# A Newton attention stage in an order of one period per quad, with scores of four heads in three parts

## The chip, the core and the metric

The kernel runs on one core of one Trainium2 chip. The metric is the device time of one execution in microseconds (us); lower is better. A profile of one execution gives every instruction's start and duration on the engines: PE (TensorE, with PEld for its weight loads), ACT (ScalarE), DVE (VectorE), POOL (GpSimd) and SP (SyncE, which issues DMAs).

## What is computed

The input x has 8 batch rows of 512 tokens of 128 numbers, all float32. First comes an attention of a special kind; then six layers of windowed attention and a feed-forward network, which the change leaves alone. The first part of the reference, cut:

```python
s = einsum('bhnd,bhmd->bhnm', Q, K) * scale        # 16 heads of 8, 512 x 512, causal
lam = s_masked.max(-1) + 1.0
for _ in range(4):                                 # Newton passes
    d = maximum(lam[..., None] - s, EPS)
    w = where(mask, 1 / d, 0)
    f = w.sum(-1) - 1
    fp = -where(mask, 1 / d**2, 0).sum(-1)
    lam = lam - f / fp
p = where(mask, 1 / maximum(lam[..., None] - s, EPS), 0)
o = einsum('bhnm,bhmd->bhnd', p / p.sum(-1), V)
x = x + o.reshape(b, n, d) @ Wo.T                  # with Q, K, V from layernorm(x)
```

## The kernel before

Three functions run one after the other: `stage1` (the part above), `stage2` (the six layers) and `stage3` (copies the result out). Only `stage1` is of interest.

**Tiling.** A batch row is worked off in four *quads* of four heads (32 quads in all). The causal scores of one head, 512 x 512, are kept as four *units* u of 128 query tokens with 128 (u + 1) keys: 128, 256, 384 and 512 columns, 1280 together (`ROW`), in the order `UORD = (3, 2, 0, 1)`. A quad has 4 x 1280 columns on 128 partitions.

**Work of a quad.** TensorE projects queries and keys (`project`, into psM) and ScalarE copies them to qT and kT. TensorE forms lam - s (`differences`, into psD): head h sits in rows 32h to 32h + 8 of qT and kT, so the heads of a quad are in different row groups of the array; the masks are added by bf16 multiplications. VectorE reads the scores into S and takes their minimum (`scores_in`), which gives the first lam. Then four Newton passes: ScalarE takes the reciprocal square root of lam - s, unit by unit, since lam is a bias for each row (`roots`, line 541); GpSimd squares the result of heads 0 to 2 (`squares`, line 646) and ScalarE that of head 3 (line 547); VectorE takes count, mean and variance of 1/d with `bn_stats` (`moments`, line 732), from which both sums follow, and updates lam in seven small dependent steps (`small`, lines 751 to 766). After pass 4 lam is transposed (line 768) and SP sends it by four small DMAs into a row of qT (`send_lam`, line 251), so that TensorE can form the *final* differences with keys on the partitions (line 354). ScalarE takes their root out of psD (`roots_final`, line 556), GpSimd squares it (`weights`, line 651), TensorE multiplies with the values (`weigh`, line 399, into psO), ScalarE copies to oq (line 564), TensorE transposes, VectorE divides (`quad_out`). When the four quads of a row are done, the row turns: transposition of attn, output projection, residual, layer norm for stage 2, transposition, store. The layer norm of the next row's input is done meanwhile.

**Order.** Each engine has one strict queue. `stage1` writes it by *slots*: 24 slots a row; slot s does one pass of one quad (`OFFSET = (0, 5, 8, 13, 16, 21)` gives the slots of score, passes 1 to 4 and final within a quad, 6 slots apart from quad to quad), with the other work placed at slot numbers by hand. psD holds two heads (2 x 1280 columns, five banks), so `differences` runs in two *pairs*, and the second pair waits until the first has been read. W has two buffers (`WBUF`), S four. On VectorE the steps of `small` stand between the statistics of the next pass, one after each unit.

Of the kernel before, what the change touches and what calls it, by code (L numbers as in the profile page):

```python
# [18 lines left out]
P = 128  # L19
# [7 lines left out]
QUAD = 4  # L27
# [35 lines left out]

POFF = ({3: 0, 2: SEQ, 0: SEQ + UNIT[2], 1: 2 * SEQ},
        {1: ROW, 3: 3 * SEQ, 2: 4 * SEQ, 0: 4 * SEQ + UNIT[2]})
KLEN = [SEQ - k * P for k in range(NBLK)]
KOFF = [{k: POFF[i][3 - k] for k in range(NBLK)} for i in range(2)]
# [4 lines left out]
NSLOT = 24  # L74
LAST = ITERS + 1
OFFSET = (0, 5, 8, 13, 16, 21)
SLOTS = {}
for _j in range(NQ):
    for _p in range(LAST + 1):
        SLOTS[(6 * _j + OFFSET[_p]) % NSLOT] = (_j, _p, (6 * _j + OFFSET[_p]) // NSLOT)  # L80
WBUF = {1: 0, 2: 1, 4: 0, 5: 1}
SMALLS = (1, 7, 7, 7, 8)


def stage1(nc, x, consts, w1qk, w1vo, x1d, hist):
    with ExitStack() as ctx:
# [27 lines left out]
        S = sb("S", [P, NQ, QUAD, ROW])  # L114
        W = sb("W", [P, 2, QUAD, ROW])
# [4 lines left out]
        stats = sb("stats", [P, 2, NU, 6])  # L120
        inv = sb("inv", [P, NU])
        lam = sb("lam", [P, NQ, 32])
        lamT = sb("lamT", [P, 4, 32])
# [6 lines left out]
        psD = ps("psD", [P, 2 * ROW])  # L130
# [17 lines left out]
        lam_in = [sem(f"lam_in{i}") for i in range(4)]  # L148
        s_d = sem("s_d")
        s_half = sem("s_half")  # L150
        s_s = sem("s_s")
        s_root = sem("s_root")
        s_rootf = sem("s_rootf")
        s_w = sem("s_w")
        s_w3 = sem("s_w3")
        s_wf = sem("s_wf")
        s_stat = sem("s_stat")
        s_small = sem("s_small")
        s_pv = sem("s_pv")
        s_oq = sem("s_oq")  # L160
        s_turn = sem("s_turn")
        s_rden = sem("s_rden")
        s_attn = sem("s_attn")
        s_m = sem("s_m")
        s_mev = sem("s_mev")
        s_x1 = sem("s_x1")
        s_ln = [sem("s_ln_in"), sem("s_ln_out")]
        s_rs = [sem("s_rs_in"), sem("s_rs_out")]
        s_fix = [sem("s_fix_in"), sem("s_fix_out")]
        s_ap = [sem("s_ap_in"), sem("s_ap_out")]  # L170
        held = {e: sem(f"held1_{e}") for e in ("pe", "act", "pool", "dve", "sp")}

        M_PRO, M_B = 3, 13
        E_PRO, E_B = 3, 12
        FIX = 7

# [3 lines left out]
        def live(b, s):  # L180
            return not isinstance(b, int) or 0 <= b - SLOTS[s][2] < BATCH

        def prev(b, s, passes=range(LAST + 1), buf=None):
            while True:
                b, s = (b, s - 1) if s else (b - 1, NSLOT - 1)
                if isinstance(b, int) and b < 0:
                    return None
                if live(b, s) and SLOTS[s][1] in passes and (buf is None or WBUF[s % 6] == buf):
                    return b, s


        def before(b, s):
            p = SLOTS[s][1]
            return ago(b, s, OFFSET[p] - OFFSET[p - 1])


        def ago(b, s, n, passes=range(LAST + 1)):
            b, s = (b, s - n) if s >= n else (b - 1, s - n + NSLOT)
            if isinstance(b, int) and b < 0 or not live(b, s) or SLOTS[s][1] not in passes:
                return None  # L200
            return b, s

        def rank(b, s, passes, quad=None):
            def fits(t):
                return SLOTS[t][1] in passes and (quad is None or SLOTS[t][0] == quad)
            if isinstance(b, int) and b == 0:
                return sum(fits(t) for t in range(NSLOT) if t < s or not live(b, t))
            return b * sum(fits(t) for t in range(NSLOT)) + sum(fits(t) for t in range(s) if live(b, t))  # L210

        def junk(passes, quad=None):
            return sum(SLOTS[t][1] in passes and (quad is None or SLOTS[t][0] == quad) for t in range(NSLOT) if SLOTS[t][2])

        NEWTON = range(1, LAST)
        FINAL = (LAST,)
        FIRST = (0,)
        ARRAY = (0, LAST)
        SENT = (ITERS,)

        def due(t):
            return t + 1 if SLOTS[t][1] else t + 3.5

        def smalls(b, s):
            ups = [t for t in range(NSLOT) if SLOTS[t][1] < LAST]
            if isinstance(b, int) and b == 0:
                return sum(SMALLS[SLOTS[t][1]] for t in ups if due(t) < due(s) or not live(b, t))
            return b * sum(SMALLS[SLOTS[t][1]] for t in ups) + \  # L230
                sum(SMALLS[SLOTS[t][1]] for t in ups if due(t) < due(s) and live(b, t))

        @block.sync
        def _(sp):
# [11 lines left out]
            def send_lam(b, s):  # L246
                j = SLOTS[s][0]
                sp.wait_ge(s_small, smalls(b, s) + SMALLS[ITERS])
                sp.sem_inc(held["sp"], 1)
                for q in range(4):  # L250
                    sp.dma_start(qT[DH1:P:32, j, :].rearrange("h (u q p) -> h u q p", u=NBLK, q=4)[:, :, q, :],
                                 lamT[32 * q:32 * q + NU, j, :]).then_inc(lam_in[j], 16)

            def store_x1(b):
                sp.wait_ge(s_x1, b + 1)
                sp.sem_inc(held["sp"], 1)
                sp.dma_start(tokens(x1d, b - 1), x1[:, :, :]).then_inc(x1_out, 16)

            def store_h(i, n_ev):
                sp.wait_ge(s_mev, n_ev)  # L260
                sp.sem_inc(held["sp"], 1)
                sp.dma_start(hist[bass.ds(i, 1)].rearrange("a p n -> (a p) n"), houtT[:, :]).then_inc(hist_out, 16)

            def body(b):
                first = isinstance(b, int) and b == 0
                second = isinstance(b, int) and b == 1
                tail = isinstance(b, int) and b == BATCH
                for s in range(NSLOT):

                    t = ago(b, s, 1, SENT)  # L270
                    if t is not None:
                        send_lam(*t)
                    if s == 0 and not first:
                        sp.wait_ge(s_x1, b)
                        sp.sem_inc(held["sp"], 1)
                        sp.dma_start(xres[:, :, :], tokens(x, b - 1)).then_inc(xres_in, 16)
                    if s == 1 and not tail:
                        sp.wait_ge(s_ap[0], b + 1)
                        sp.sem_inc(held["sp"], 1)
                        if isinstance(b, int) and b == BATCH - 1:  # L280
                            sp.sem_inc(xin_in, 16)
                        else:
                            sp.dma_start(xin[:, :, :], tokens(x, b + 1)).then_inc(xin_in, 16)
                    if s == 5 and not first and not second:
                        store_h(b - 2, b * E_B + E_PRO + 1)
                    if s == 23 and not first:
                        store_x1(b)

            body(0)
            body(1)  # L290
            with sp.Fori(2, BATCH - 1) as b:
                body(b)
            body(BATCH - 1)
            body(BATCH)
            store_h(BATCH - 1, BATCH * E_B + E_PRO + 3)
            sp.wait_ge(x1_out, 16 * BATCH + 32)
            sp.wait_ge(hist_out, 16 * BATCH + 32)

        @block.tensor
        def _(pe):  # L300
            def m_free(n_ev):
                pe.wait_ge(s_mev, n_ev)
                pe.sem_inc(held["pe"], 1)

            def project(which, j, n_ev, n_x1=None):
                if n_x1 is None:
                    m_free(n_ev)
                else:
                    pe.wait_ge(s_x1, n_x1)
                    pe.sem_inc(held["pe"], 1)  # L310
                pe.matmul(psM[:, :], wqk[:, which, j, :], hT[:, :], start=True, stop=True).then_inc(s_m, 1)

            def turn_h(n_ev, n_ap):
                pe.wait_ge(s_ap[0], n_ap)
                pe.sem_inc(held["pe"], 1)
                m_free(n_ev)
                for k in range(NBLK):
                    mm = pe.transpose(psM[:, k * P:(k + 1) * P], hin[:, k, :], ident[:, :])
                mm.then_inc(s_m, 1)
# [3 lines left out]
            def differences(b, s, pair):  # L323
                j, p, back = SLOTS[s]
                if pair == 0 and p:
                    pe.wait_ge(lam_in[j], 64 * (rank(*before(b, s), SENT, j) + 1))
                    pe.sem_inc(held["pe"], 1)
                elif pair == 0 and not (j == 0 and isinstance(b, int) and b == 0):
                    pe.wait_ge(s_mev, b * E_B + E_PRO + (2 * j + 1 if j else 0))
                    pe.sem_inc(held["pe"], 1)  # L330
                heads = (2 * pair, 2 * pair + 1)


                def free(i):
                    t = (b, s) if pair else prev(b, s, ARRAY)
                    if t is None:
                        return
# [1667 lines left out]
```

## Time and profile before

| | us |
|---|---|
| median of 3 runs | 5497.16 |
| lowest, highest | 5484.47, 5499.78 |
| the profiled execution, its own time | 5491.38 |
| its span, first to last instruction | 5489.6 |
| busy in the span: PE, DVE, POOL, ACT | 4505.2, 4021.2, 3451.4, 3029.9 |

The span is what the engines saw; a little lies around it. Busy time is a sum over three stages with different limits, so a stage has to be read from stretches of its own. The PE clock is the clock that was granted to TensorE as a share of 2.4 GHz; its levels are 1.2 and 2.4 GHz.

### The profile page before, as it was taken

The numbers are of one execution on the slowest core, as the hardware profiler recorded it, in microseconds if no ns is written. First come the engines' busy times: TensorE is split into PE (matmuls) and PEld (weight loads), VectorE is DVE, ScalarE is ACT, GpSimd is POOL, SyncE is SP. The second block draws the span as 40 slices with busy tenths as digits, with TensorE's granted clock in tenths as the row PEclk, the third lists the DMA queues.
The fourth block names the chain that finished last, engine by engine and source line by source line (L and its number), as shares of the span: only waits on it lengthen the run. The fifth ranks groups of instructions, "written<-read, shape, count | busy, mean of one in ns | idle before, by whom it ended". The sixth has DMA issues, their size and how long they took to land. (4 is left out here: it accounts for less than half of the span.)

```text
span 5489.6 us, 155667 instructions
## 1 busy us (share of the span) xinstructions
PE 4505.2 (82%) x60088; PEld 2421.4 (44%) x60088; DVE 4021.2 (73%) x7142; ACT 3029.9 (55%) x4257; POOL 3451.4 (63%) x1662
## 2 busy tenths in 40 slices
PE   4676666766666658999999899999999899989995
PEld 2333333333333325554555455544555455545553
DVE  6666675656666638887888788878888788878883
ACT  5667676766777634554555444544555455545551
POOL 4556665656656646666666666666666566656662
PEclk9755555555555569999999999999999999999997
DMA  0000000000000014444444444444444444444443
GB/s 11 5 1 8 7 2 7 2 8 0 8 5 2 6 39 115 106 106 109 114 106 108 114 107 104 106 117 98 106 106 105 99 110 109 110 108 115 106 106 86
DMA packets 234292, 382.56 MB, mean 70 GB/s; under 512 B 38433, under 2 KB 63777, under 8 KB 233505
## 3 DMA queue, kind: packets, MB, share of 16 engines
q1 hardware_dynamic: 229408, 371.06, 28.7%
q8 instruction: 488, 8.00, 0.6%
q10 hardware_dynamic: 4224, 2.10, 0.1%
q14 instruction: 172, 1.40, 0.1%
HBM read 51.89 MB, written 18.87 MB: 13 GB/s over the span
## 5 line engine op out<-in xcount | busy, mean ns | idle before, releaser
L732 DVE BATCH_NORM_STATS2 stats<-W 128x6 f32<-128x512 f32 (+3 forms) x2048 | 863.6, 478 | 565.5 <-POOL W L646 565.4
L646 POOL TENSOR_TENSOR W<-W 128x1280 f32<-128x1280 f32 x384 | 881.5, 2319 | 512.8 <-ACT W L541 510.0
L541 ACT ACTIVATE W<-S,lam 128x512 f32<-128x512 f32 (+3 forms) x2048 | 946.6, 551 | 123.7 <-DVE lam L766 90.1
L1557 POOL TENSOR_TENSOR m<-m 128x1024 f32<-128x1024 f32 x384 | 902.5, 2362 | 67.6 <-DVE m L1665 67.4
L1174 PE MATMUL pb<-xs,wg 128*128 128x512 f32 x1536 | 768.4, 635 | 51.4 <-DMA xs<-hist 36.8
L1563 POOL TENSOR_TENSOR sm<-sm,mx 128x1024 f32<-128x1024 f32 x192 | 451.9, 2354 | 511.6 <-DVE mx L1679 511.6
L1688 DVE SCALAR_TENSOR_TENSOR nf<-rn,m 128x1024 f32<-128x1024 f32 x384 | 616.1, 1636 | 99.2 <-ACT rn L1419 76.0
L351 PE MATMUL psD<-kT,qT 9*128 9x384 f32 (+3 forms) x1024 | 410.6, 767 | 322.2 <-DVE S L719 176.0
L1410 ACT ACTIVATE lnn<-pb,cst 128x1024 f32<-128x1024 f32 x192 | 213.8, 1114 | 814.5 <-PE pb L1181 814.5
L1405 ACT ACTIVATE sq<-pb 128x1024 f32<-128x1024 f32 x384 | 381.9, 1021 | 509.8 <-PE pb L1174 509.8
L354 PE MATMUL psD<-qT,kT 9*128 9x512 f32 (+3 forms) x1024 | 407.5, 763 | 266.0 <-ACT WF L556 142.9
L1553 POOL TENSOR_TENSOR sqs<-sq 128x1024 f32<-128x1024 f32 x192 | 456.9, 2379 | 228.3 <-ACT sq L1405 228.3
L1568 POOL TENSOR_TENSOR pr<-pr,rsum 128x1024 f32<-128x1024 f32 x192 | 407.3, 2121 | 306.8 <-DVE rsum L1701 304.4
L1664 DVE TENSOR_TENSOR m<-pb,tab 128x1024 f32<-128x1024 f32 x384 | 464.6, 1210 | 15.5 <-ACT sq L1405 12.4
L1665 DVE TENSOR_TENSOR m<-pb,tab 128x1024 f32<-128x1024 f32 x384 | 465.5, 1212 | 0.0
L351 PEld LDWEIGHTS psD<-kT,qT 9*128 9x128 f32 x1024 | 230.0, 317 | 521.2 <-issue 509.7
L1174 PEld LDWEIGHTS pb<-xs,wg 128*128 128x128 f32 x1536 | 292.9, 201 | 363.7 <-issue 356.7
L651 POOL TENSOR_TENSOR WF<-WF 128x1280 f32<-128x1280 f32 x128 | 294.1, 2319 | 239.5 <-ACT WF L556 239.5
L1181 PE MATMUL pb<-sqs,ones 128*128 128x512 f32 x768 | 394.8, 638 | 29.8 <-DVE m L1665 22.9
L354 PEld LDWEIGHTS psD<-qT,kT 9*128 9x128 f32 x1024 | 228.9, 315 | 416.8 <-issue 405.8
L1230 PE MATMUL pb<-pT,vr 64*64 64x32 f32 x12288 | 335.7, 221 | 65.6 <-issue 65.6
L1246 PE MATMUL pb<-wg,xs 128*128 128x512 f32 x768 | 372.8, 608 | 20.1 <-issue 17.7
(120 smaller groups left out, 7559.2 us busy)
## 6 DMA issues: line engine op xcount, KB each, us to landing
qkn<-nf SPq DMA_DIRECT2D x1536, 128.0 KB, 2.4
vr<-v SPq DMA_DIRECT2D x96, 768.0 KB, 6.0
vr<-v SPq DMA_DIRECT2D x96, 192.0 KB, 5.5
xr<-hist SPq DMA_DIRECT2D x48, 256.0 KB, 2.9
hist<-xo SPq DMA_DIRECT2D x48, 256.0 KB, 4.0
wg<-wqkv SPq DMA_DIRECT2D x24, 384.0 KB, 3.6
xs<-hist SPq DMA_DIRECT2D x48, 128.0 KB
vr<-v SPq DMA_DIRECT2D x96, 64.0 KB, 6.2
```

The source lines that it names most:

```text
L351: pe.matmul(psD[:, c:c + UNIT[u]], qT[r, j, u * P:(u + 1) * P], kT[r, j, 0:UNIT[u]], start=fresh, stop=True, skip_group_check=True)
L354: pe.matmul(psD[:, c:c + UNIT[u]], kT[r, j, k * P:(k + 1) * P], qT[r, j, k * P:SEQ], start=fresh, stop=True, skip_group_check=True)
L541: ins = nc.scalar.activation(W[:, buf, h, c], S[:, j, h, c], ACT.Abs_reciprocal_sqrt, bias=lam[:, j, i:i + 1])
L646: nc.gpsimd.tensor_tensor(W[:, buf, h, :], W[:, buf, h, :], W[:, buf, h, :], ALU.mult).then_inc(s_w, 1)
L732: ins = nc.vector.bn_stats(out=stats[:, buf, i, :], in_=W[:, buf, h, UOFF[u]:UOFF[u] + UNIT[u]])
L1174: mm = pe.matmul(out[:, half, :], wg[:, g, c:c + P], xs[:, 0:SEQ], start=True, stop=True)
L1553: nc.gpsimd.tensor_tensor(sqs[:, :, :], sq[:, :, 0, :], sq[:, :, 1, :], ALU.add).then_inc(s_sqs, 1)
L1557: nc.gpsimd.tensor_tensor(m1[:, which, :, :], m1[:, which, :, :], m2[:, which, ::-1, :], ALU.add)\
L1563: nc.gpsimd.tensor_tensor(x, x, mx[:, :].unsqueeze(2).broadcast_to([P, 16, 64]), ALU.subtract).then_inc(s_sub, 1)
L1664: nc.vector.tensor_tensor(m1[:, which, :, :], src[:, :, :], tab[:, which, 0, :, :], ALU.mult)
L1665: nc.vector.tensor_tensor(m2[:, which, :, :], src[:, :, :], tab[:, which, 1, :, :], ALU.mult)\
L1688: nc.vector.scalar_tensor_tensor(out=nf[:, which, :, :], in0=rn[:, which, :].unsqueeze(1).broadcast_to([P, 2, SEQ]), scalar=1e12, in1=m1[: ...
```

## The change

Only `stage1` and its tables change.

- **Order.** The slots go. The loop body is now written once per quad ("period") on every engine, `for j in range(NQ)`, with each step at a fixed place and a *lag*: `quad(b, j, lag)` is the quad that entered `lag` periods ago. Scores and pass 1 belong to lag 0, passes 2 and 3 and half of pass 4 to lag 1, the rest of pass 4 to lag 2, the final part to lag 3, the row's turn to lag 4. The places are the result of a search over orders.
- **Scores of four heads at a time, in three parts.** `PARTS = ((3,), (2, 0), (1,))`: unit 3 of all four heads (512 columns, a bank each), then units 2 and 0 (384 + 128, a bank each), then unit 1 (256, two heads in a bank, in two halves with a wait on `s_half` between). `take` waits for a bank's last user. `scores_in`, `root_final`, `weights` and `weigh` follow the same parts; `root_final` and `weights` take four heads in an instruction.
- **A buffer per pass.** W and stats have one buffer for each of the four passes; S has two instead of four.
- **Squares.** Pass 4 (`p = 3`) is squared by GpSimd for all four heads; in the other passes ScalarE still squares head 3.
- **Updates.** The steps of an update (`update`) stand behind each other and no longer between statistics.
- **Values** are projected a quad at a time (4 products of 32 columns) and not for the whole row.
- Most work has semaphores of its own (`s_root[p]`, `s_up[p]`, ...) instead of shared ones with computed ranks.

```diff
-NSLOT = 24
-OFFSET = (0, 5, 8, 13, 16, 21)
-WBUF = {1: 0, 2: 1, 4: 0, 5: 1}
+PARTS = ((3,), (2, 0), (1,))
+BANKS = ((0, 1, 2, 3), (4, 0, 1, 2), (3, 4))
+SQP = ((0, 1, 2), (0, 1, 2), (0, 1, 2), (0, 1, 2, 3))
+SQA = ((3,), (3,), (3,), ())
...
-        S = sb("S", [P, NQ, QUAD, ROW])
-        W = sb("W", [P, 2, QUAD, ROW])
+        S = sb("S", [P, 2, QUAD, ROW])
+        W = sb("W", [P, ITERS, QUAD, ROW])
-        psD = ps("psD", [P, 2 * ROW])
+        psD = ps("psD", [P, 5, SEQ])
...
+                if part < 2:
+                    for u in PARTS[part]:
+                        for h in range(QUAD):
+                            unit(h, u)
...
+                else:
+                    for i in range(2):
+                        if i == 1:
+                            pe.wait_ge(s_halff if final else s_half, at(n))
+                            pe.sem_inc(held["pe"], 1)
+                        unit(i, 1)
+                        unit(2 + i, 1)
+                        mask(i, 1, 1)
+                        mm = mask(2 + i, 1, 1)
...
+            def root_final(q, part):
...
+                if part == 0:
+                    ins = nc.scalar.activation(WF[:, :, 0:SEQ], psD[:, 0:4, :], ACT.Abs_reciprocal_sqrt, bias=zero[:, 0:1])
```

One period on ScalarE, and then on GpSimd. The conditions `if live(...)` and `if last(...)` ahead of each step are left out; they only drop steps of quads that do not exist.

```diff
+                        queries(quad(b, j, 0))
+                        root(quad(b, j, 2), 3, 2)
+                        root_final(quad(b, j, 3), 0)
+                        keys(quad(b, j, 0))
+                        root(quad(b, j, 1), 1, 0)
+                        root(quad(b, j, 2), 3, 3)
+                        root(quad(b, j, 1), 1, 1)
+                        turned_attn(quad(b, j, 4))
+                        root(quad(b, j, 1), 1, 2)
+                        root(quad(b, j, 1), 1, 3)
+                        square(quad(b, j, 1), 1, 3)
+                        root_final(quad(b, j, 3), 1)
...
+                        values(quad(b, j, 0))
...
+                        root(quad(b, j, 1), 2, 0)
...
```

```diff
+                        square(quad(b, j, 0), 0, 0)
+                        weights(quad(b, j, 3), 2)
+                        square(quad(b, j, 0), 0, 1)
+                        square(quad(b, j, 0), 0, 2)
+                        square(quad(b, j, 1), 3, 0)
+                        square(quad(b, j, 1), 3, 1)
+                        square(quad(b, j, 1), 3, 2)
+                        weights(quad(b, j, 2), 0)
+                        square(quad(b, j, 0), 1, 0)
+                        square(quad(b, j, 0), 1, 1)
+                        square(quad(b, j, 0), 1, 2)
+                        square(quad(b, j, 1), 3, 3)
+                        weights(quad(b, j, 2), 1)
+                        square(quad(b, j, 0), 2, 0)
...
```

TensorE at the head of the loop, before: the first pair of score blocks of a quad, two heads in turn, unit by unit (the reads name kT and qT; `L342` rows are waits).

```order
L342 ISA
L351 MATMUL psD<-kT,qT 128x512
L342 REGISTER_ALU
L351 MATMUL psD<-kT,qT 128x512
L351 MATMUL psD<-kT,qT 128x384 x2
L351 MATMUL psD<-kT,qT 128x128 x2
L351 MATMUL psD<-kT,qT 128x256
L360 MATMUL psD<-cmaskb,identb 128x128
L360 MATMUL psD<-cmaskb,identb 128x256
```

The same place of the changed kernel: part 0 of the final differences of the quad three periods back (`L371`), the key projection (`L337`), part 0 of the new quad's scores (`L374`).

```order
L371 MATMUL psD<-qT,kT 128x512 x4
L381 MATMUL psD<-cmaskb,identb 128x128 x4
L327 ISA
L337 MATMUL psM<-hT,wqk 128x512
L327 REGISTER_ALU
L363 REGISTER_ALU
L374 MATMUL psD<-kT,qT 128x512 x4
L381 MATMUL psD<-cmaskb,identb 128x128 x4
```

A block of one unit now covers four heads, and blocks of two quads alternate part by part where whole arrays followed each other.

VectorE in the loop, before: statistics of a pass with the update of another quad between them.

```order
L732 BN_STATS stats<-W 128x6
L741 REGISTER_ALU
L754 TENSOR_TENSOR psX<-psX,stats 128x16x2
L732 BN_STATS stats<-W 128x6
L741 REGISTER_ALU
L757 TENSOR_TENSOR psX<-psX,stats 128x16x2
L732 BN_STATS stats<-W 128x6
L741 REGISTER_ALU
L759 TENSOR_REDUCE psX<-psX 128x32
```

The changed kernel, from the reading of part 0 (`L840`) through the statistics and the update of pass 2 to the statistics of pass 4's last head.

```order
L840 TENSOR_SCALAR S,psX<-psD 128x512 x4
L849 BN_STATS stats<-W 128x6 x16
L865 TENSOR_TENSOR psX<-stats,psX 128x16x2
L867 TENSOR_TENSOR psX<-psX,stats 128x16x2
L869 TENSOR_TENSOR psX<-psX,stats 128x16x2
L871 TENSOR_REDUCE psX<-psX 128x32
L873 RECIPROCAL inv<-psX 128x16
L875 SCALAR_TENSOR_TENSOR psX<-psX,inv 128x16
L878 TENSOR_TENSOR lam<-lam,psX 128x16
L849 BN_STATS stats<-W 128x6 x4
```

The seven steps have moved together, behind all sixteen statistics of their own pass.

GpSimd in the loop, before: three squares of a pass (`L646`), then the final weights of a pair of heads (`L651`).

```order
L646 TENSOR_TENSOR W<-W 128x1280
L645 REGISTER_ALU
L646 TENSOR_TENSOR W<-W 128x1280
L650 REGISTER_ALU
L651 TENSOR_TENSOR WF<-WF 128x1280
L650 REGISTER_ALU
L651 TENSOR_TENSOR WF<-WF 128x1280
```

The changed kernel: the weights of part 2, squares of passes 1 and 4, the weights of part 0, squares of pass 2 and the fourth square of pass 4.

```order
L740 TENSOR_TENSOR WF<-WF 128x4x256
L733 REGISTER_ALU
L734 TENSOR_TENSOR W<-W 128x1280
L733 REGISTER_ALU
L734 TENSOR_TENSOR W<-W 128x1280 x4
L739 REGISTER_ALU
L740 TENSOR_TENSOR WF<-WF 128x4x512
L734 TENSOR_TENSOR W<-W 128x1280 x3
L733 REGISTER_ALU
L734 TENSOR_TENSOR W<-W 128x1280
```

The weights come in pieces of four heads and stand between squares of three different passes.

## Rows read from the trace of the kernel before

**Rows 1.** The page: granted clock of TensorE in 40 slices of the span, tenths.

```profile
PEclk9755555555555569999999999999999999999997
```

**Rows 2.** Stretches: start:end length, busy us (count) of PE, PEld, DVE, ACT, POOL; clock, DMA.

```profile
511.50:564.80 53.30, 39.20 (x132) 20.16 (x132) 37.98 (x129) 40.76 (x77) 36.67 (x17) 0.51 0.00 1
...
621.00:691.10 70.10, 44.07 (x156) 24.90 (x156) 37.78 (x134) 42.67 (x81) 36.33 (x24) 0.56 0.04 12
449.80:691.10 241.30, 162.28 (x556) 86.02 (x556) 154.97 (x530) 168.67 (x316) 149.73 (x79) 0.53 0.02 5
2009.50:5489.60 3480.10, 3193.55 (x55616) 1733.17 (x55616) 2775.74 (x2888) 1671.67 (x1729) 2249.27 (x1015) 0.96 0.46 107
```

**Rows 3.** Timeline (start, us, engine, line): ScalarE's first and last copy of oq.

```profile
208.00 0.56 ACT L564 COPY oq<-psO 128x512 f32<-128x512 f32 x1
...
1992.10 0.58 ACT L564 COPY oq<-psO 128x512 f32<-128x512 f32 x1 [7.00 <-PE psO L399]
```

**Rows 4.** Waits in 449.8 to 691.1, one batch row: us in total, times, longest.

```profile
DVE stats L732 <- POOL W L646: 72.8, 25, 9.2
...
ACT qT L497 <- PE psM L311: 13.8, 4, 4.5
ACT vals L506 <- PE psM L414: 12.7, 1, 12.7
ACT W L541 <- DVE lam L766: 10.9, 3, 4.0
```

**Rows 5.** Timeline of ScalarE: keys, final roots, roots of four heads, a square.

```profile
1031.34 0.67 ACT L502 ACTIVATE kT<-psM,fixed 128x512 f32<-128x512 f32 x1
1031.91 2.53 ACT L556 ACTIVATE WF<-psD,zero 128x1280 f32<-128x1280 f32 x2
1034.33 7.34 ACT L541 ACTIVATE W<-S,lam 128x512 f32<-128x512 f32 x16
1041.70 1.27 ACT L547 ACTIVATE W<-W 128x1280 f32<-128x1280 f32 x1
```

**Rows 6.** Timeline of VectorE: scores of two heads begun, sixteen statistics, a whole update.

```profile
1005.20 0.67 DVE L719 TENSOR_SCALAR_CACHE_REDUCE S<-psD 128x512 f32<-128x512 f32 x1
...
1006.95 0.72 DVE L719 TENSOR_SCALAR_CACHE_REDUCE S<-psD 128x512 f32<-128x512 f32 x1
...
1011.32 6.39 DVE L732 BATCH_NORM_STATS2 stats<-W 128x6 f32<-128x512 f32 x16
...
1034.03 0.20 DVE L751 TENSOR_TENSOR psX<-stats,psX 128x32 f32<-128x32 f32 x1
...
1035.57 0.17 DVE L766 TENSOR_TENSOR lam<-lam,psX 128x16 f32<-128x16 f32 x1
```

**Rows 7.** GpSimd: squares in the timeline; a stage 2 group (busy, mean ns | idle).

```profile
1037.86 13.87 POOL L646 TENSOR_TENSOR W<-W 128x1280 f32<-128x1280 f32 x6
...
L1557 POOL TENSOR_TENSOR m<-m 128x1024 f32<-128x1024 f32 x384 | 902.5, 2362 | 67.6 <-DVE m L1665 67.4
```

**Rows 8.** Timeline of TensorE: projection, score blocks, one block alone, masks, values.

```profile
17.91 2.05 PE L311 MATMUL psM<-hT,wqk 128*128 128x512 f32 x2 [0.77 <-ACT hT L497]
...
23.64 4.60 PE L351 MATMUL psD<-kT,qT 9*128 9x512 f32 x14 [0.87 <-ACT kT L502]
...
29.25 1.19 PE L351 MATMUL psD<-kT,qT 9*128 9x256 f32 x2
...
1021.60 0.93 PE L360 MATMUL psD<-cmaskb,identb 128*128 128x128 bf16 x7
...
1040.68 4.50 PE L399 MATMUL psO<-WF,vals 128*32 128x512 f32 x32
```

**Rows 9.** SP and DMA: lam sent, another DMA's landing, first issue of stage 2.

```profile
1027.97 2.27 SPq L251 DMA_DIRECT2D qT<-lamT  x4
...
qkn<-nf SPq DMA_DIRECT2D x1536, 128.0 KB, 2.4
...
2009.50 0.35 SPq L997 DMA_DIRECT2D ident<-consts  x1
```

More of the change, by code:

```diff
@@ L192, in before @@
[L192 to L231, printed above, removed]
+        def quad(b, j, lag):
+            c = j - lag
+            return b * NQ + c, c % NQ, b - (-(c // NQ))
@@ new lines, in live, with last, at, of @@
+        def live(b, j, lag):
+            return not isinstance(b, int) or 0 <= b * NQ + j - lag < QUADS
+        def last(b, j, lag):
+            return (j - lag) % NQ == NQ - 1 and live(b, j, lag)
+        Q_MADE, Q_OUT, K_MADE, K_OUT, V_MADE, V_OUT = range(6)
+        TURNED, TURNED_OUT, SUMMED, ADDED = range(4)
+        def at(n, k=0, per=1):
+            return per * n + (per * NQ + k + 1)
+        def of(r, k=0, per=1):
+            return per * r + (per + k + 1)
+        def norm(r, step):
+            return of(r, step, NORMED + 1)
@@ new lines, in body @@
+            def body(b):
+                for j in range(NQ):
+                    if live(b, j, 0):
+                        send_lam(quad(b, j, 0))
+                    if last(b, j, 1):
+                        store_x1(quad(b, j, 1)[2])
+                        if not isinstance(b, int) or quad(b, j, 1)[2] + 1 < BATCH:
+                            load_xres(quad(b, j, 1)[2] + 1)
+                    if last(b, j, 3):
+                        store_h(quad(b, j, 3)[2])
+                    if j == 2 and (not isinstance(b, int) or b + 2 <= BATCH):
+                        load_xin(b + 2)
@@ new lines, in project, with values @@
+            def project(q, which):
+                n, j, r = q
+                if which == 0 and j == 0:
+                    pe.wait_ge(s_thev, of(r))
+                    pe.sem_inc(held["pe"], 1)
+                pe.matmul(psM[:, :], wqk[:, which, j, :], hT[:, :], start=True, stop=True).then_inc(s_qkv, 1)
+            def values(q):
+                n, j, r = q
+                for k in range(NBLK):
+                    mm = pe.matmul(psM[:, k * 32:(k + 1) * 32], hT[:, k * P:(k + 1) * P], wvo[:, 0, j * 32:(j + 1) * 32],
+                                   start=True, stop=True)
+                mm.then_inc(s_qkv, 1)
@@ L327, in differences, with score @@
+            def score(q, part, final):
+                n, j, r = q
+                if part == 0 and final:
+                    pe.wait_ge(lam_in[j], of(r, 63, 64))
                     pe.sem_inc(held["pe"], 1)
[L328 to L329 removed]
+                elif part == 0:
+                    pe.wait_ge(s_qkv, at(n, Q_OUT, 6))
                     pe.sem_inc(held["pe"], 1)
[L331 removed]
```

986 lines of the change are left out of this document (529 added, 457 removed).

## The prediction

> **What bounds the kernel now.** I read the stretches first, then the waits, then the durations. The kernel has a first stage (stieltjes attention, 8 rows of 4 quads) that ends at 2009.5 us and a second and third stage that take the other 3480.1 us [rows 2, 9]. The diff touches the first stage alone, so 3480.1 us stand, and with them the clock of that part (0.96 granted, against about 0.53 in the first stage, that is the 1.2 GHz level nearly all the time [rows 1, 2]).
>
> In the first stage the copies of a finished quad (oq) come at 208.0 for the first and 1992.1 for the last [rows 3]. One row of four quads takes 241.3 us, 60.3 a quad. In it ScalarE is busy 168.7, TensorE 162.3, VectorE 155.0, GpSimd 149.7 us [rows 2]. No engine is full: even ScalarE idles 72.6 us, 18 a quad. The waits say where [rows 4]: VectorE waits 72.8 us for GpSimd's squares; ScalarE waits 13.8 us for the query projections, 12.7 us for the value projection and 10.9 us for an updated lam. The projections themselves are short (2.05 us [rows 8]); they stand in TensorE's one queue behind score blocks that wait for psD. So the bound is the order in which four strict queues meet, not an engine. The four quads of a row are uneven too: the last one takes 70.1 us, the other three 57.1 in the mean ((241.3 - 70.1) / 3), and a quiet one 53.3 [rows 2].
>
> **The prices.** All from rows.
> ScalarE: 16 root instructions (4 heads) take 7.34 us, 1.84 a head; the square of a head 1.27 [rows 5]. So an instruction costs (1.84 - 1.27) / 3 = 0.19 and a column 0.84 ns. The final roots, two of 1280 columns in 2.53 [rows 5], become pieces of 2048, 512 + 1536 and 1024 columns: 1.92, 2.10, 1.05, sum 5.07, as before (4 x 1.27).
> VectorE: statistics of 4 heads in 6.39, 1.60 a head; reading a head's scores 1006.95 - 1005.20 = 1.75 (the four parts about 0.60, 0.52, 0.25, 0.38); a lam update whose seven steps stand one behind the other 1.71 (1034.03 to 1035.74) [rows 6].
> GpSimd: six squares in 13.87, 2.31 each [rows 7].
> TensorE: a block of 256 columns in one row group takes 1.19 us, that is 3.33 ns a column and 0.34 once. Seven blocks of two heads (1280 and 1024 columns) take 4.60: exactly 1280 x 3.33 ns + 0.34, so the two row groups run side by side, each at its own pace. Masks cost 0.93 for seven [rows 8].
>
> **The change part by part.**
> 1. *Scores of four heads at a time.* A part of 512 columns: 1.71 + 0.34 + four masks 0.6 = 2.7 us; the 384 + 128 part 3.0; the 256 part, in two halves with a wait between, 3.1. Sum 8.8 an array of scores, against two pairs of about 7.3 (4.60 + 0.93 + 1.19 and some 0.6 for the last mask and the seams) = 14.6 before [rows 8]. It saves some 11 us of TensorE a quad; what lies beside it is the work of the other three engines, and TensorE is not in the chain below. That four groups run abreast is not in the rows for row groups; the nearest row is the product with the values, where four column groups take 4.50 us for 1280 columns each (1280 x 3.33 ns + 0.24) [rows 8].
> 2. *Pass 4 squared by GpSimd alone.* ScalarE loses 1.27 us a quad, GpSimd gains 2.31. ScalarE: 168.7 / 4 = 42.2, minus 1.27: 40.9 a quad. GpSimd: 37.4 + 2.3 = 39.7.
> 3. *Updates no longer interleaved with statistics.* VectorE: 16 x 1.60 + 4 x 1.75 + 4 x 1.71 = 39.4, plus about 2.4 for the transposition, the output of a quad and the norms (estimate, from the 38.7 a quad that the row holds now): 41.8 a quad. This step costs VectorE about 3 us; before, the steps hid between statistics.
> 4. *A buffer per pass, the new orders.* They remove nothing and set the period. I laid one period out, zero being ScalarE's query copy. ScalarE: copy, root (pass 4, head 2) to 2.4, final root of part 0 to 4.4, keys 5.1, root (pass 2, head 0) 6.9, root (pass 4, head 3) 8.8. GpSimd: square of pass 4 head 2 from 2.5 to 4.8, part 0 of the final weights (2048 columns, 3.7) to 8.5, then three squares of pass 2 to 10.8, 13.1, 15.4. VectorE: statistics of head 2 to 17.0, head 3 to 18.6, update to 20.35. ScalarE, which would be free at 18.0, waits for this lam until 20.4; from there to the end it has ten roots (pass 3 four, pass 1 four, pass 4 two: 18.4), two squares (2.5), the last part of the final root (1.05) and the quad's copy (0.56), 22.6 together: 43.0. With the hand-overs 43.3 us. GpSimd and TensorE fit: the quad's copy ends at 37.9; its transposition 1.1, the query projection 2.1 and the final scores of part 0 (2.7) end at 44.0, 0.7 into the next period, where ScalarE wants them at 2.4.
> So the chain of a period is: root, GpSimd's square, GpSimd's weights, three squares, two statistics, one update, then ScalarE without a gap. It replaces 57 to 60.
> 5. *The row turn.* The residual, the norms' statistics and three copies. Before, a turn costs 70.1 - 57.1 = 13 us over the others; the bound below is nothing. Its longest wait, 12.7 us for the value projection of the whole row, is gone, since each quad now projects its own quarter; residual and norm still pass through all queues in series. So I take 4.8 a row, 1.2 a quad.
> 6. *GpSimd's weights in pieces of four heads.* They cost at least 1.81 ns a column as the squares do (2.31 / 1280); other two-operand work of 1024 columns on GpSimd takes 2362 ns, 2.31 ns a column [rows 7]. That would lengthen part 0 by 1.0 us, on the chain. I take half, 0.5.
> Mean period: 43.3 + 1.2 + 0.5 = 45.0 us.
> 7. *SP's queue.* Each quad sends lam with four DMAs, 2.27 us of issue [rows 9]; SP waits for that update first in each period and only then stores x1 and loads the next rows. Landing is not shown for them; for a DMA of 128 KB it is 2.4 us. The update of pass 4 ends near 35, lands near 40 and is wanted at 41.3: hidden by 1.3 us, and 1.7 more before ScalarE feels it. The loads of x have a whole row.
>
> **The sum.** The first projection starts at 17.9 as before [rows 8]. A Newton pass alone takes 1.84 + 3 x 2.31 + 2 x 1.60 + 1.71 = 13.7. Period 0 (projections, three parts of scores, their reading 7.0, one pass): 33. Period 1 (two passes and the third begun): 36. Period 2: 40. Periods 3 to 31: 29 x 45.0 = 1305. Then the emptying pipeline: 36, 16 and 19. Behind the last copy 2009.5 - 1992.1 = 17.4 [rows 3, 9]. Together 18 + 33 + 36 + 40 + 1305 + 36 + 16 + 19 + 17 = 1520, against 2009.5. Plus 3480.1 is a span of 5000. The profiled execution took 5491.4 with a span of 5489.6, so 1.8 lie around it: **5002 us**. That execution is 5.8 under the median of the runs (5497.2), which is inside their spread.
>
> **The rivals.**
> - *The order closes tighter.* The wait of 2.4 us for lam shrinks, the turn is hidden: ScalarE alone, 41 to 42 a quad. 29 x 3 = 87 less: 4915. For it: its busy time is 40.9. Against it: VectorE needs 41.8 and cannot run ahead.
> - *The four heads take turns on TensorE.* The multiplications would start in program order; each is recorded as two passes, and the second waits for the first in the same row group, so a part of 512 columns takes 4 x 0.85 + 0.85 + 0.34 + 0.6 = 5.2 instead of 2.7. Then keys, scores and their reading enter the chain: about 1.5 a period, 44 in all: 5046. Against it: 4.60 us is what two independent groups give; in turns the same seven blocks would need about 5.4 [rows 8]. The Trainium skill ("TensorE: Matmul & The Clock Gate", section "Step-by-step: what each phase is for") says just that matmuls stay in program order and only weight loads are pulled ahead; by that rule the time would be 5046, by the row 5002. Its section "The mechanism" draws four row groups as starting almost together; the row of 4.60 bears out that part for two groups.
> - *The row turn costs what it costs now,* 13 instead of 4.8: 7.25 rows of 4 periods x 8.2 = 60 more, 5062. For it: the turn still sends two norms through all four queues in series.
> - *The orders close badly.* ScalarE now loses 18 us a quad to waits; if half of that stays, the period is 50 and the time 5002 + 29 x 5 = 5147. For it: both ScalarE and VectorE are then within 3 us of full, and a delay on one is a delay of the other, with strict queues.
> - *Slower: the round trip of lam.* The final scores of a quad stand ahead of the key projection in TensorE's queue. If the DMAs of lam took L us from the update to the scores, the loop update - L - scores 2.7 - final root to update is about 35 + L us. It decides above L = 9 and makes the kernel slower than before from a period of 62, L = 27: 5002 + 29 x 17.5 = 5510. Against it: 2.27 us of issue and 2.4 of landing [rows 9].
>
> **How the numbers follow.** Forecast (period 44 to 46.5) 0.55; tighter 0.08; heads in turns 0.10; costly row turn 0.14; orders closing badly 0.11; lam slower than before 0.02. The range goes from 4925 (the tighter case nearly whole) to 5105 (turn and half of the bad case), and leaves out some 0.17. Within 0.3% (16 us, about what a measurement of this kernel can tell) of before no case lies; I keep 0.01. Faster 0.97, slower 0.02.
>
> **What would show it.** In the new profile: copies of oq 44 to 46 us apart, over 48 at the turns of rows; the first stage ending near 1520; ScalarE above 90% busy with one wait of about 2 us a quad, for lam at pass 3; VectorE near 93%; blocks of 4 heads x 512 columns in 2.1 us (4.6 if they take turns); the weights' part 0 in 3.7 (4.7 by the other price); the second stage 3480 long. A second stage of another length, or ScalarE waiting for TensorE at the final roots, would make the prediction wrong at its base.

## The result, and the profile after

The changed kernel takes 4943.68 us (median of 4 runs, 4938.53 to 4948.72); the kernel before took 5490.82 beside it (4 runs, 5468.62 to 5499.78). The ratio is 0.901, 95% interval 0.898 to 0.904: some 547 us less. The profiled execution took 4938.53 us with a span of 4936.4. The forecast was 5002, in a range of 4925 to 5105: the time lies inside, 58 us under it.

The page of the changed kernel: busy tenths of four engines and the granted clock in 40 slices. The first 12 slices are the first stage.

```profile
PE   3666666666647999899999999899998999899995
DVE  6999999999956888788878888788887888788883
ACT  5999999999953555445544555455544555455441
POOL 4999999999965676666766676567665766576661
PEclk9755555555558999999999999999999999999997
```

From the second slice to the eleventh three engines now stand at 9, and TensorE, still at the 1.2 GHz level there as in [rows 1], at 6. The stretches have the same columns as [rows 2]: a row's turn period, an ordinary period, the row of four quads that begins with them, and the part behind the first stage.

```profile
986.80:1032.40 45.60, 31.23 (x160) 15.95 (x160) 41.73 (x141) 44.18 (x88) 40.67 (x25) 0.57 0.04 12
1032.40:1074.90 42.50, 28.83 (x140) 12.65 (x140) 38.56 (x126) 39.52 (x77) 38.34 (x16) 0.50 0.00 1
986.80:1159.90 173.10, 115.57 (x580) 52.61 (x580) 159.62 (x530) 162.74 (x315) 157.90 (x79) 0.53 0.02 7
1479.40:4936.40 3457.00, 3179.03 (x55616) 1725.73 (x55616) 2775.45 (x2888) 1672.50 (x1729) 2249.30 (x1015) 0.97 0.46 108
```

A row takes 173.1 us where it took 241.3 [rows 2]. ScalarE, VectorE and GpSimd do about the work they did (162.7, 159.6, 157.9 us), so their idle time is what went: ScalarE's from 72.6 to 10.4 us a row. TensorE does 46.7 us less a row; what that is worth, the run `pairs` below shows.

Timeline of ScalarE (start, us): copies of a finished quad, and SP's first DMA issue of the next stage, as in [rows 3] and [rows 9].

```profile
166.49 0.57 ACT L615 COPY oq<-psO 128x512 f32<-128x512 f32 x1
...
1031.94 0.57 ACT L615 COPY oq<-psO 128x512 f32<-128x512 f32 x1
...
1074.38 0.56 ACT L615 COPY oq<-psO 128x512 f32<-128x512 f32 x1
...
1378.16 0.57 ACT L615 COPY oq<-psO 128x512 f32<-128x512 f32 x1
...
1461.26 0.58 ACT L615 COPY oq<-psO 128x512 f32<-128x512 f32 x1 [3.25 <-PE psO L425]
...
1479.44 0.35 SPq L1142 DMA_DIRECT2D ident<-consts  x1
```

Between the first copy and that at 1378.16 lie 28 periods, 43.27 us each; within a row they are 42.4, 42.4, 42.6 and 45.6. The first stage ends at 1479.4 instead of 2009.5: 530.1 of the span's 553.2 us. The other 23.1 us are in code that is the same, 3457.0 instead of 3480.1 [rows 2]. In the traces of all the runs below this part is between 3449 and 3469 us, and by and large it goes with the time in which TensorE stands at 1.2 GHz in it (265 us in the profile before, 221 after, 220 to 247 in the others, from the mean granted clock of this part). The change does not touch this code. Why the profile before is the longest of all here, no run shows; only the 530 us of the first stage are counted for the change below.

The waits in the row from 986.8 to 1159.9 (us in total, times, longest), against [rows 4]:

```profile
ACT W L585 <- DVE lam L878: 7.9, 4, 2.8
...
DVE stats L849 <- POOL W L734: 4.0, 7, 0.6
...
ACT vals L544 <- PE psM L342: 0.9, 2, 0.5
```

VectorE waited 72.8 us a row for GpSimd's squares and waits 4.0; ScalarE's waits for the projections, 26.5 together, are 0.9; what it still waits for is lam, once a quad (7.9 of its 10.4 us). So the wait for lam closes the chain. The timeline of one ordinary period on ScalarE, then VectorE, GpSimd and TensorE (in brackets: the idle time before, and who ended it):

```profile
1037.19 0.57 ACT L530 COPY qT<-psM 128x512 f32<-128x512 f32 x1
1037.66 1.93 ACT L585 ACTIVATE W<-S,lam 128x512 f32<-128x512 f32 x4
...
1041.90 9.16 ACT L585 ACTIVATE W<-S,lam 128x512 f32<-128x512 f32 x20
1051.09 1.27 ACT L592 ACTIVATE W<-W 128x1280 f32<-128x1280 f32 x1
...
1057.55 7.34 ACT L585 ACTIVATE W<-S,lam 128x512 f32<-128x512 f32 x16 [2.38 <-DVE lam L878]
1064.92 1.27 ACT L592 ACTIVATE W<-W 128x1280 f32<-128x1280 f32 x1
1066.13 3.73 ACT L585 ACTIVATE W<-S,lam 128x512 f32<-128x512 f32 x8
```

```profile
1052.41 3.25 DVE L849 BATCH_NORM_STATS2 stats<-W 128x6 f32<-128x512 f32 x8 [0.61 <-POOL W L734]
1055.69 0.21 DVE L865 TENSOR_TENSOR psX<-stats,psX 128x32 f32<-128x32 f32 x1
...
1057.18 0.17 DVE L878 TENSOR_TENSOR lam<-lam,psX 128x16 f32<-128x16 f32 x1
```

```profile
1037.38 4.61 POOL L734 TENSOR_TENSOR W<-W 128x1280 f32<-128x1280 f32 x2 [0.63 <-ACT W L585]
1041.94 3.60 POOL L740 TENSOR_TENSOR WF<-WF 128x2048 f32<-128x2048 f32 x1
1045.50 9.15 POOL L734 TENSOR_TENSOR W<-W 128x1280 f32<-128x1280 f32 x4
```

```profile
1042.16 2.09 PE L374 MATMUL psD<-kT,qT 9*128 9x512 f32 x8 [2.20 <-ACT kT L536]
1044.19 0.61 PE L381 MATMUL psD<-cmaskb,identb 128*128 128x128 bf16 x4
```

From the query copy at 1037.19 the chain runs through the root at 1037.66, GpSimd's square, its weights (3.60 us), three more squares, VectorE's statistics of two heads and one update, to the roots at 1057.55: 20.36 us. Behind that ScalarE has no gap until the next query copy. TensorE's block of four heads by 512 columns takes 2.09 us, the price of one head's 512 columns (512 x 3.33 ns + 0.34 us = 2.05, by the slope of [rows 8]).

### The profile page after: what moved, and what is told of

Same layout as the page of the kernel before. It is cut to its first block and busy times, and to the rows that moved or that the text cites. A ratio compares the mean times of both kernels' runs of the same rounds, so it can differ in the third digit from the quotient of the medians.

```text
span 4936.4 us, 154683 instructions
## 1 busy us (share of the span) xinstructions
PE 4103.4 (83%) x60260; PEld 2147.1 (43%) x60260; DVE 4056.8 (82%) x7132; ACT 2979.7 (60%) x4240; POOL 3516.9 (71%) x1655
## 5 line engine op out<-in xcount | busy, mean ns | idle before, releaser
L734 POOL TENSOR_TENSOR W<-W 128x1280 f32<-128x1280 f32 x416 | 954.9, 2319 | 141.2 <-ACT W L585 139.9
L849 DVE BATCH_NORM_STATS2 stats<-W 128x6 f32<-128x512 f32 (+3 forms) x2048 | 832.4, 478 | 57.6 <-POOL W L734 56.5
L1853 DVE COPY oT<-pb 128x512 f32<-128x512 f32 x384 | 246.6, 683 | 176.5 <-PE pb L1375 176.5
L374 PE MATMUL psD<-kT,qT 9*128 9x512 f32 (+3 forms) x1024 | 201.8, 747 | 191.0 <-DVE S L840 107.3
L1342 PEld LDWEIGHTS pb<-qkn 64*32 64x32 f32 x24576 | 260.3, 105 | 203.0 <-issue 202.2
L1401 PE MATMUL pb<-oT,wo 128*128 128x512 f32 x768 | 344.4, 602 | 1.5 <-DVE oT L1853 1.5
L1375 PEld LDWEIGHTS pb<-pT,v 64*64 64x64 f32 x12288 | 255.8, 135 | 191.8 <-issue 191.8
```

What stands on the lines that cost most here:

```text
L734: nc.gpsimd.tensor_tensor(W[:, p, h, :], W[:, p, h, :], W[:, p, h, :], ALU.mult).then_inc(s_wp[p], 1)
L849: ins = nc.vector.bn_stats(out=stats[:, p, h * NBLK + u, :], in_=W[:, p, h, UOFF[u]:UOFF[u] + UNIT[u]])
L1375: mm = pe.matmul(out[64 * b:64 * b + 64, s, o:o + WIN], src[64 * s:64 * s + 64, k, c:c + DH2], pT[64 * s:64 * s + 64, b, r:r + WIN], start ...
```

## Is the chain the bound? Four runs with work added

Theory A: the period is that chain, and the engines' waits outside it are real slack. Theory B: all three engines are so full that work anywhere lengthens the period. Four kernels add the same operations on data of their own, once a period: a square of 1280 columns on ScalarE, three statistics on VectorE, a product of 512 columns on GpSimd.

```diff
+ nc.scalar.activation(spareo[:, :], spare[:, :], ACT.Square)
+ for i in range(3):
+     nc.vector.bn_stats(out=spare6[:, i, :], in_=spare[:, 0:SEQ])
+ nc.gpsimd.tensor_tensor(sparep[:, :], spare[:, 0:SEQ], spare[:, 0:SEQ], ALU.mult)
```

**slack_all** puts all three where the engines have slack: behind the value copy, behind the statistics of head 2 in pass 4 (`moments(..., 3, 2)`), and behind the weights of part 1.

> The changed kernel with extra work of no use in each period, on three engines: ScalarE squares 1280 columns (1.2 us) between the value copy and the roots of pass 3, VectorE takes statistics of 512 columns three times (1.8 us) at the end of its period, GpSimd multiplies 512 columns (0.9 us) before its squares of pass 3. Theory A (one chain through the three engines sets the period of 42.4 us; ScalarE's wait of 2.4 us for lam, VectorE's waits of 1.2, 0.6 and 0.6 us, GpSimd's wait of 1.3 us are real slack): the period stays at 42.4 to 42.5 us, the total grows by 0 to 10 us, most of it at the turns of rows. Theory B (ScalarE and VectorE are simply full, at 93% busy): a period grows by 1.2 to 1.8 us, the total by 35 to 55 us.

Measured: 4955.5 us, ratio 0.903 [0.902, 0.905], 11.8 us over the changed kernel; the first stage 13.7 longer. That is a little more than the 0 to 10 expected, and not at the turns of rows. The copies of its row:

```profile
1041.42 0.58 ACT L619 COPY oq<-psO 128x512 f32<-128x512 f32 x1
...
1083.88 0.58 ACT L619 COPY oq<-psO 128x512 f32<-128x512 f32 x1
...
1127.95 0.57 ACT L619 COPY oq<-psO 128x512 f32<-128x512 f32 x1
```

One ordinary period is 42.5 as before; the next is 44.1 instead of 42.4, and only this one grows. It is the one in which VectorE also takes the norm statistics of the next row's input. So some 4.2 us of work (1.25, 1.88 and 1.04) is free in three periods of four: theory A, with the slack used up in the fourth, where VectorE has most to do.

**act_chain**, **dve_chain** and **pool_chain** put one of the three each into the chain: the square behind `square(..., 2, 3)`, in ScalarE's stretch behind lam; the statistics between the last `moments` of pass 2 and its update; the product between the weights of part 0 and the three squares.

> The changed kernel; the same extra square of ScalarE (1.2 us) placed a little later, behind the square of pass 3, inside the stretch that theory A counts as chain. Theory A: the period grows by all of it, to 43.6 us, the total by 36 us. A rival chain through GpSimd alone would let it pass for less than 10 us.

> The changed kernel; the same three extra statistics of VectorE (1.8 us) placed between the last statistics of pass 2 and the update of lam. Theory A: all of it enters the period, 44.2 us, the total grows by 56 us. If VectorE's own busy time (about 39.7 of 42.4 us) was the limit, the first 2.7 us would be free wherever they stand: 0 to 10 us.

> The changed kernel; the same extra product of GpSimd (512 columns, 0.9 us) placed between the final weights of part 0 and the squares of pass 2. Theory A: the chain runs there through GpSimd, the period grows by 0.9 us to 43.3, the total by 28 us, though GpSimd idles 4 us a period. Rival (GpSimd at 91% is not in the chain): 0 to 5 us.

| | ordinary period | first stage | time, ratio to before |
|---|---|---|---|
| after | 42.4 | 1479.4 | 4943.7, 0.901 |
| slack_all | 42.5 | 1493.1 | 4955.5, 0.903 |
| act_chain | 43.6 | 1514.6 | 4976.1, 0.908 |
| dve_chain | 44.1 | 1532.2 | 4984.6, 0.909 |
| pool_chain | 43.4 | 1502.1 | 4960.6, 0.905 |

Each lengthens every ordinary period by nearly the added operation's own time (1.25, 1.88, 1.04): 1.2, 1.6 and 1.0 us. The same square on ScalarE costs 35.2 us at one place and at most 13.7 at another, with two more operations beside it there. The period is the chain. One limit: in the turn period the product on GpSimd costs nothing (45.6), so there the chain goes another way, and the first stage grew by 22.7 us where 28 was expected.

## The square of pass 4

**pass4_act** undoes this part alone: ScalarE again squares head 3 of pass 4.

```diff
-SQP = (..., (0, 1, 2, 3))
+SQP = (..., (0, 1, 2))
-SQA = ((3,), (3,), (3,), ())
+SQA = ((3,), (3,), (3,), (3,))
 # ScalarE
 square(quad(b, j, 1), 1, 3)
+square(quad(b, j, 2), 3, 3)
 # GpSimd
-square(quad(b, j, 1), 3, 3)
```

> The changed kernel with one part undone: head 3 of pass 4 is squared by ScalarE again (1.2 us, behind its square of pass 2) and not by GpSimd (2.3 us less there). Theory A (that place is in front of ScalarE's wait of 2.4 us for lam, and GpSimd's fourth square lies behind the ones the chain needs): period 42.4 to 42.5 us, total within 8 us of the changed kernel. Rival (giving ScalarE's work to GpSimd is what shortens the period): 43.6 us, total 36 us more.

Measured: 4947.8 us, ratio 0.902 [0.900, 0.904], the first stage 2.5 us longer, periods 42.5, 42.4, 42.6 and 45.9. The move is worth at most 3 us: ScalarE's 1.27 fit into the 2.38 us in which it waits for lam, and GpSimd's 2.31 lie behind the squares on which lam depends.

**before_pool4** makes the same move alone in the kernel before.

```diff
-                if pair == 1:
+                if pair == 1 and p != ITERS:
                     # ScalarE squares head 3
 # GpSimd, behind the other squares of pass 4
+                    nc.gpsimd.tensor_tensor(W[:, buf, 3, :], W[:, buf, 3, :], W[:, buf, 3, :], ALU.mult).then_inc(s_w4, 1)
```

> The kernel before with only one part of the change: GpSimd squares all four heads of pass 4. A pass alone then ends with GpSimd's fourth square, 1.84 + 4 x 2.31 = 11.1 us after its start and not 8.8, and in the slot order the next slots wait for it. Expected: slower by 20 to 75 us (0.6 to 2.3 us a quad). Rival (ScalarE is relieved where it is short): faster by up to 40 us.

Measured: 5451.7 us, ratio 0.994 [0.992, 0.996]: faster by some 32 us, where I expected slower. Four of its periods take 238.5 us in the mean instead of 241.1, and its waits in one row are, among others:

```profile
POOL WF L655 <- ACT WF L557: 19.0, 6, 4.4
...
PE psD L355 <- ACT WF L557: 14.2, 4, 5.6
```

The same two waits of the kernel before, in 449.8 to 691.1:

```profile
POOL WF L651 <- ACT WF L556: 29.1, 8, 6.0
...
PE psD L354 <- ACT WF L556: 16.8, 4, 6.9
```

I had counted GpSimd's square as the longer one and not asked what stood behind ScalarE's. That the final roots, which free psD, come earlier without it fits these waits, but no run takes it apart. Neither is it all: about 25 of the 32 us are in the first stage.

**pass2_act2** tries to use the result. If head 2 of pass 2 is squared by ScalarE too, which waits there anyway, GpSimd's part of the chain is a square shorter.

```diff
-SQP = (..., (0, 1, 2), ...)   # pass 2
+SQP = (..., (0, 1), ...)
 # ScalarE
 root(quad(b, j, 1), 1, 2)
+square(quad(b, j, 1), 1, 2)
 # GpSimd
-square(quad(b, j, 0), 1, 2)
```

> The changed kernel with one square more on ScalarE where it has slack: head 2 of pass 2 is squared by ScalarE (1.2 us in front of its wait of 2.4 us) and not by GpSimd, whose third square of pass 2 ends the chain's GpSimd piece. Theory A: statistics of head 2 no longer wait for GpSimd, lam of pass 2 comes 0.6 us earlier, the period falls to 41.8 us, the total by 12 to 20 us. Theory B (engines full): ScalarE has more work, the period grows by up to 1.2 us, the total by up to 36 us.

Measured: 4952.2 us (4931.8 to 4960.3), ratio 0.902 [0.900, 0.905]; the period 42.5, the first stage 1.8 us longer. A miss. ScalarE, VectorE and TensorE in it:

```profile
1038.30 0.58 ACT L530 COPY qT<-psM 128x512 f32<-128x512 f32 x1
...
1053.51 1.27 ACT L592 ACTIVATE W<-W 128x1280 f32<-128x1280 f32 x1
...
1055.26 1.53 ACT L604 ACTIVATE WF<-psD,zero 128x1536 f32<-128x1536 f32 x1
...
1058.37 7.34 ACT L585 ACTIVATE W<-S,lam 128x512 f32<-128x512 f32 x16 [1.43 <-DVE lam L878]
...
1067.32 3.73 ACT L585 ACTIVATE W<-S,lam 128x512 f32<-128x512 f32 x8 [0.31 <-DVE lam L856]
...
1054.82 1.67 DVE L849 BATCH_NORM_STATS2 stats<-W 128x6 f32<-128x512 f32 x4 [0.32 <-ACT W L592]
...
1056.93 2.09 PE L374 MATMUL psD<-kT,qT 9*128 9x384 f32 x16 [0.75 <-ACT WF L604]
```

The last statistics now wait for ScalarE's square of head 3. In the changed kernel that square ends at 1051.09 + 1.27 = 1052.36, 15.2 us behind the query copy, at about the same time as GpSimd's third (the statistics that waited for it begin at 1052.41). Here it ends at 1054.78, 16.5 behind the query copy of 1038.30: the moved square stands in front of it and lengthens this strand as it shortens the other. So lam of pass 2 comes 20.07 us behind the query copy instead of 20.36, 0.3 earlier and not 0.6. That gain is lost again further on. The final root of part 1 (L604), which stands behind the squares, now ends 18.5 us behind the query copy instead of 17.2; TensorE waits 0.75 us for it with part 1 of the new scores, and ScalarE waits 0.31 us for the first lam that comes of them, which it does not in the changed kernel.

## The scores of four heads

**pairs** keeps the new order and forms parts 0 and 1 two heads at a time.

```diff
-for u in PARTS[part]:
-    for h in range(QUAD):
-        unit(h, u)
+for pair in ((0, 1), (2, 3)):
+    for u in PARTS[part]:
+        for h in pair:
+            unit(h, u)
+    # and the masks of the pair here
```

> The changed kernel with the scores of parts 0 and 1 formed for heads 0 and 1, masks, then heads 2 and 3, masks, as pairs before; orders, banks and buffers stay. A part of 512 columns then takes about 4.9 us and not 2.7. By the trace of the changed kernel the final scores of part 0 end 1.4 us ahead of ScalarE's use and the new scores have some 1.3 us until they delay VectorE in the chain; the delays of both add to about 3.4 us at VectorE's first reading. Expected: period 44.0 to 44.6 us, total 45 to 65 us more. Rival (TensorE is 65% busy in this stage and off the chain): no change.

Measured: 5106.4 us, ratio 0.932 [0.930, 0.933]; period 48.1, the first stage 164 us longer. The direction was right, the size 2.5 to 3.6 times what I expected. One period as a stretch, then TensorE, VectorE and ScalarE in the one before it:

```profile
1199.40:1247.60 48.20, 37.25 (x143) 15.64 (x142) 40.26 (x137) 39.78 (x77) 39.01 (x17) 0.50 0.01 2
```

```profile
1158.80 2.08 PE L374 MATMUL psD<-kT,qT 9*128 9x512 f32 x4 [0.91 <-ACT kT L537]
...
1166.42 2.07 PE L371 MATMUL psD<-qT,kT 9*128 9x384 f32 x8 [2.89 <-DVE S L841]
...
1163.57 0.69 DVE L841 TENSOR_SCALAR_CACHE_REDUCE S<-psD 128x512 f32<-128x512 f32 x1 [3.63 <-PE psD L381]
...
1180.43 0.56 DVE L841 TENSOR_SCALAR_CACHE_REDUCE S<-psD 128x384 f32<-128x384 f32 x1 [4.63 <-PE psD L381]
...
1187.73 3.73 ACT L586 ACTIVATE W<-S,lam 128x512 f32<-128x512 f32 x8 [3.58 <-DVE lam L857]
```

A pair of heads takes 2.08 us, four heads take 2.09: half the work costs the same. TensorE is busy 37.25 of 48.2 us, and yet it waits. psD has five banks, so TensorE fills a part, VectorE reads it, TensorE fills the next. In the changed kernel VectorE waits 1.20 us for part 0; here it waits 3.63 and 4.63, and the chain becomes this loop: scores, reading, scores, reading, the first lam, for which ScalarE waits 3.58. **pairs_part0** and **pairs_part1** do one part each (the same edit under `if part == 0` or `if part == 1`).

> As the run with scores in pairs, but for part 0 alone (512 columns; final and new scores); part 1 stays at four heads. Theory C (the loss of 5.7 us a period with pairs comes from a chain TensorE - VectorE - TensorE in which both parts stand twice): with part 0 alone VectorE's first reading comes 3.3 us later, of which 1.3 us are slack: period 44.2 to 45.0 us, first stage 60 to 80 us longer. Rival (TensorE's queue as a whole is full and each part costs by its time): 45.3 us for each part alone.

> The same for part 1 alone (384 + 128 columns). Theory C: the final scores of part 1 and then the new ones end 2.0 us later each; in the changed kernel VectorE's reading of part 1 has 1.0 us of slack, and the first lam comes only 0.3 us ahead of ScalarE's use, so about 3 us enter the period: 44.9 to 45.7 us, first stage 75 to 100 us longer. If only part 0 lay in the chain, as I had assumed for the run with pairs, this one would cost less than 0.5 us a period.

Measured: 4979.6 us, ratio 0.909 [0.906, 0.912], the first stage 34.5 longer (period 42.6 to 44.2, 43.5 in the mean); and 5046.0, ratio 0.921 [0.917, 0.924], 102.3 longer (45.3 to 46.5). Part 1 costs three times part 0, so the rival by which each costs the same, 45.3, is out for part 0. For part 0 I expected 60 to 80, too much, and for part 1 75 to 100, a little too low. In TensorE's order part 1 stands twice between VectorE's two readings, as final scores and as scores, with the values' products between; part 0 stands twice too, but in the changed kernel ScalarE and VectorE each have over 1 us of slack there. That fits the sizes, and no run takes it apart. Together the two make 137; the other 27 come only with both.

So the four row groups running abreast are worth 164 us in this order, though TensorE is the least busy engine and wasn't in the chain that I had laid out. With pairs the kernel is still 377 us faster than before (5106.4 against 5483.8 beside it). That rest belongs to the new order, the buffers, the updates and the values by the quad; of these only pass 4's square and the fourth buffer were tried alone, and no run separates the others.

## The buffer per pass

**share_w** lets passes 1 and 3 use one buffer of W (three in all).

```diff
+BUF = (0, 1, 0, 2)
-W = sb("W", [P, ITERS, QUAD, ROW])
+W = sb("W", [P, 3, QUAD, ROW])
-act.wait_ge(s_stat[p], at(n - 1, h, QUAD))
+act.wait_ge(s_stat[2 if p == 0 else p], at(n - 1, h, QUAD))
```

> The changed kernel with three buffers of W and not four: passes 1 and 3 share one; a root of pass 1 then waits for the statistics of pass 3 of the quad before. By the trace of the changed kernel those statistics end before each of the four roots starts (by 0.9 us or more). Theory A: period 42.4 to 42.5 us, first stage within 5 us. Rival (a buffer for every pass is part of the gain): a longer period by 1 us or more, 30 us in all.

Measured: 4936.8 us, ratio 0.901 [0.899, 0.904], the first stage 1479.7. No cost, as expected: the fourth buffer buys nothing. Whether three are needed was not tried.

## Why the prediction was right, point by point

| | predicted | measured |
|---|---|---|
| to the first copy | 127 + 37.9 | 166.5 |
| 28 periods | 28 x 45.0 = 1260 | 1211.7 |
| last three copies | 78 | 83.1 |
| behind the last copy | 17.4 | 18.2 |
| first stage | 1520 | 1479.4 |
| the rest | 3480.1 | 3457.0 |

(The row of the 28 periods and that of the last three copies split the sum of the prediction at measured copies.)

- **What bounds the kernel before:** right. The gain is idle time between four strict queues, ScalarE's 62 us a row.
- **The period itself:** under the forecast case. I gave 44 to 46.5 us, with copies over 48 apart at the turns; the mean is 43.27, ordinary periods are 42.4 and turns 45.6. The time lies in the range because the range took in most of the tighter case too.
- **The chain:** right. ScalarE waits for lam 2.38 us (2.4 laid out), and goes on 20.36 us after the query copy (20.4). That this agrees to the hundredth is luck: the update ended at 1057.35, 20.16 behind the copy where I had 20.35, and the hand-over of 0.2 stood elsewhere in my sum. Four runs show that this chain is the period.
- **ScalarE's stretch behind lam:** over by 0.8 us, and with the small change ahead of it the ordinary period by 0.9 (43.3 against 42.4), 24 us in all. I summed durations, 22.6, and added 0.3 for hand-overs. Neighbours overlap by about 0.1 us instead: the square of 1.27 lasts 1.21 or 1.16 from start to start, the query copy of 0.57 lasts 0.47, and the starts from 1057.55 to the next query copy add up to 22.1.
- **GpSimd's weights:** I took half of the surcharge of two different operands, +0.5 us. Part 0 took 3.60 us, 1.76 ns a column, the price of a square. The product's operands are the same, and the row with that property was [rows 7]'s first. Over by 14 us.
- **The row turn:** 173.1 - 4 x 42.43 = 3.4 us, predicted 4.8. Over by 10 us. These three terms are the 48 us of the periods.
- **VectorE:** I had it busy 41.8 us a quad and used this against the tighter case; it is 39.9 (159.6 a row). The updates were to cost it 3 us; the row shows 1.2 more than before.
- **The emptying:** 5 us short, the start and end within 2. ScalarE waits up to 5.0 us for final scores there (at 1437.2), which I had at nothing.
- **Four heads abreast:** right, 2.09 us (2.05). The rival that they take turns is out: in the block at 1042.16 four multiplications start 7 ns apart, the other four 1.0 us later, and all end within 2.09. The Trainium skill ("TensorE: Matmul & The Clock Gate", section "Step-by-step: what each phase is for") says that matmuls stay in program order. Read as heads in turns the block would have taken 4.6 us, and the trace does not bear out that reading; the order of the starts it does not contradict. Its section "The mechanism" draws four row groups as starting almost together, and here the trace agrees, 7 ns.
- **The other rivals:** *tighter* was the nearest, since ordinary periods are 42.4, but not by its mechanism: the wait for lam stays. The *costly turn* fell with 3.4 us, the *bad closing* with ScalarE's idle time of 2.6 us a quad, and the *round trip of lam* with final scores that in the running loop never keep ScalarE waiting over 0.44 us.
- **The second stage:** taken as fixed at 3480.1; 23 us of the miss of 64 in the span. One profiled length is good to some 15 us here, and I gave the term no width.
- **What I did not see:** that the four-head blocks were needed for the chain to hold at all. I counted the 11 us of TensorE that they save a quad as nothing in the period, since TensorE was not in my chain; only the rival of heads in turns, at 44 us, touched this. `pairs` shows 164 us.

## What to carry to other kernels

Where several strict queues feed each other in a loop, lay out one period by hand from measured durations, find the one wait that closes it, and check it by adding the same small operation once inside and once outside the chain: 1.2 us a period cost 35 in one place and at most 14 in the other. Before an operation is moved off an engine or made cheaper, ask whether a second strand ends at the same moment, whether the move lengthens that one, and what stands behind it in its queue; the least busy engine can be the one that may not get slower.

## What the runs showed of the hardware that I had not expected

- Matrix products of four heads in four row groups, 9 rows each, take 2.09 us, those of two heads 2.08.
- Consecutive activations overlap by about 0.1 us (1064.92 + 1.27, the next at 1066.13): the time from start to start is what adds up, not the duration. The square, which reads what the root wrote, begins 0.03 us behind the root's end (1057.55 + 7.34, then 1064.92).
- GpSimd multiplies an operand by itself at 1.76 to 1.81 ns a column (3.60 us for 2048, 2.3 for 1280), and adds two different operands, one of them read backwards, in another stage, at 2.31 [rows 7]. No run here tells these differences apart.
- The same second stage took 3449 to 3480 us in the traces, with TensorE at the 1.2 GHz level for 220 to 265 us of it.
